# Flamingo-style gated cross-attention block on one core: the set-up becomes steps of the order tables

## The reference

```
h  = layernorm(x)
a  = ln1(h + mha(h, h, h, mask_s))              # unit A
b  = ln2(a + mha(a, ctx, ctx, mask_x))          # unit B
c  = ln3(b + relu(b @ w1 + b1) @ w2 + b2)       # C
x1 = x + tanh(g_x) * c
n  = layernorm(x1)
y  = x1 + tanh(g_f) * down(silu(gate(n)) * up(n))   # E: activations rounded to 8 bits, weights to -1, 0, 1
```

## Time and profile before

| | |
|---|---|
| median of 3 runs | 1021.93 us (1019.71 to 1024.56) |
| profiled execution | 1026.44 us, span 1024.5 us |
| PE busy | 867.8 us, 85% of the span |
| DVE busy | 788.5 us, 77% |
| ACT busy | 637.9 us, 62% |
| POOL busy | 591.2 us, 58% |
| mean granted TensorE clock | 0.934 |

### The profile page before, as it was taken

The page is one execution under the profiler, slowest core; times in us unless marked ns, Lnnn a source line. Parts: engine busy times, 40 slices in busy tenths (PEclk is TensorE's granted clock), DMA queues, the critical chain, the costliest instruction groups (busy, mean ns, idle before and its releaser), DMA issues.

```text
span 1024.5 us, 26372 instructions
## 1 busy us (share of the span) xinstructions
PE 867.8 (85%) x10089; PEld 708.1 (69%) x10147; DVE 788.5 (77%) x1903; ACT 637.9 (62%) x996; POOL 591.2 (58%) x630
## 2 busy tenths in 40 slices
PE   0327678989999999999999999999999999978565
PEld 0215457777878787878787878787878787766443
DVE  7654566668888888888888888888888888867454
ACT  1125254647677777777777767777777777764433
POOL 7004245566666666676767675757585858471520
PEclk9956696999999999999999999999999999989785
DMA  6251434343434343443444434343535352121000
GB/s 178 83 113 43 83 74 75 84 74 74 90 80 90 79 91 79 82 88 75 94 74 96 74 90 79 85 86 79 90 75 85 85 84 73 25 68 18 21 11 10
DMA packets 131755, 77.71 MB, mean 76 GB/s; under 512 B 10121, under 2 KB 131120, under 8 KB 131633
## 3 DMA queue, kind: packets, MB, share of 16 engines
q1 hardware_dynamic: 131632, 76.04, 36.7%
HBM read 54.49 MB, written 20.98 MB: 74 GB/s over the span
## 4 chain that ended last, share of the span: by engine, by line
PE 44%; DVE 16%; POOL 13%; DMA 10%; SPq 7%; issue 6%; ACT 3%; POOLq 0%; DVEq 0%; ACTq 0%
DMA stk_AQ<-parts_AQ 9%; PE lin_C L671 7%; SPq L583 6%; PE lin_A L671 4%; PE lin_E L671 4%; PE lin_B L671 4%; POOL elo L1343 3%; PE smax L750 3%; PE st L774 3%; DVE lst L1112 3%; POOL lrs L1323 2%; POOL late L1374 2%; PE smax L746 2%; POOL late L1366 2%; DVE nm_A L1162 2%
## 5 line engine op out<-in xcount | busy, mean ns | idle before, releaser
L1343 POOL TENSOR_TENSOR elo<-e,ehi 128x1024 f16<-128x1024 f32 x128 | 273.8, 2139 | 149.7 <-ACT ehi L943 149.4
L1323 POOL TENSOR_TENSOR lrs<-lve,neghalf 128x1 f32<-128x1 f32 (+1 forms) x112 | 70.9, 633 | 199.8 <-DVE lve L1121 195.5
L941 ACT ACTIVATE e<-st 128x1024 f32<-128x1024 f32 x128 | 130.1, 1017 | 45.1 <-PE st L774 44.0
L943 ACT ACTIVATE ehi<-st 128x1024 f16<-128x1024 f32 x128 | 129.8, 1014 | 0.0
L1162 DVE TENSOR_REDUCE nm_B<-smax 128x4 f32<-128x512 f32 x128 | 87.6, 684 | 20.0 <-PE smax L750 19.9
L1162 DVE TENSOR_REDUCE nm_A<-smax 128x4 f32<-128x512 f32 x128 | 87.7, 685 | 19.2 <-PE smax L750 18.5
L671 PE MATMUL lin_C<-w,late 128*128 128x256 f16 x768 | 90.0, 274 | 0.0
L671 PEld LDWEIGHTS lin_C<-w,late 128*128 128x128 f16 x768 | 75.7, 99 | 8.8
L746 PE MATMUL smax<-mb,ident_big 128*128 128x512 f16 x128 | 52.2, 408 | 18.5 <-DMA stk_AQ<-parts_AQ 9.8
L750 PE MATMUL smax<-stk_BK,stk_BQ 126*128 126x128 f16 x512 | 50.7, 222 | 9.0 <-DVE nm_B L1162 5.9
L750 PEld LDWEIGHTS smax<-stk_AK,stk_AQ 126*128 126x128 f16 x512 | 42.2, 102 | 18.3 <-issue 4.1
(11 more groups left out here) (284 smaller groups left out, 2827.3 us busy)
## 6 DMA issues: line engine op xcount, KB each, us to landing
stk_AK<-parts_AK SPq DMA_DIRECT2D x64, 128.0 KB, 4.0
stk_AQ<-parts_AQ SPq DMA_DIRECT2D x64, 128.0 KB, 5.6
stk_BK<-parts_BK SPq DMA_DIRECT2D x64, 128.0 KB, 3.7
stk_BQ<-parts_BQ SPq DMA_DIRECT2D x64, 128.0 KB, 3.7
x_a<-in_x_dram SPq DMA_DIRECT2D x16, 256.0 KB, 2.8
cx<-in_ctx_dram SPq DMA_DIRECT2D x16, 256.0 KB, 2.7
parts_AK<-qk_AK SPq DMA_DIRECT2D x16, 256.0 KB, 2.2
parts_AQ<-qk_AQ SPq DMA_DIRECT2D x16, 256.0 KB, 2.5
```

Of the source, the lines that this page charges most:

```text
L941: eng.activation(e32[:, hf, :], st[:, :], ACT.Exp, scale=SCORE).then_inc(e32_ready, 1)
L943: eng.activation(ehi[:, hf, :], st[:, :], ACT.Exp, scale=SCORE).then_inc(st_drained, 1)
L1323: eng.tensor_tensor(lrs[n][:, a:b], lve[n][:, a:b], neghalf[:, 0:b - a], ALU.pow).then_inc(ln_rstd[n], 1)
L1343: eng.tensor_tensor(elo[:, hf, :], e32[:, hf, :], ehi[:, hf, :], ALU.subtract).then_inc(elo_ready, 1)
```

## The change

- The set-up has no straight program any more but for a few constants. `PREPARE` names its steps ("set", ...), 44 of them, all of group 0, and `AT`, `LATE` and `BANK` give them places beside the first groups' steps. Each weight has its own step and its own semaphores; the first use of each result in group 0 waits for it.
- SP loads x, then two weights, the masks, the context and the others. The eight bias loads are issued by ScalarE's queue, to 22 partitions of 128 numbers instead of one row of 2816; two VectorE operations split them, and they go through DRAM into `brows`. The value-bias products are not added to the row but written into two further rows of `brows`.
- Memsets of the stacks' constant rows run over 32-bit words: a pair of f16 numbers packed in one.
- `TWEAK` adds delays to steps of single groups: 0, 1, 2 and 13, 14, 15. In group 15 the E steps get 4.97 to 8.34. All of `AT`, `START`, `LATE` and `BANK` is new.

The diff, cut to its core:

```diff
+PREPARE = (
+    [("set", n) for n in ("const", "rows", "mask", "flags", "gate", "scales")]
+    + [("set", "w", n) for n in range(10)] + [("set", "load", n) for n in range(9, 13)] + [("set", "bv", i) for i in range(2)]
+    + [("set", "stk", s, t) for s in "AB" for t in "QK"]
+    + [("set", n, m) for n in ("abs", "mean", "scale", "clip") for m in range(3)]
+    + [("set", "turn", m, r) for m in range(3) for r in range(2)]
+)
...
-START = [0.0000, 1.0125, 2.0274, 3.0405, 4.0533, 5.0678, 6.0803, 7.0946, 8.1074, 9.1216, 10.1358, 11.1490, 12.1628, 13.1762, 14.1912, 15.2043]
+START = [0.0000, 1.0188, 2.0283, 3.0470, 4.0636, 5.0814, 6.1004, 7.1147, 8.1321, 9.1501, 10.1674, 11.1867, 12.2041, 13.2212, 14.2296, 15.2538]
...
 def place(engine, item):
     g, step = item
-    if step[0] == "setup":
-        return SETUP_AT[g, step[1]]
-    return START[g] + AT[step] + LATE.get((engine, step), 0.0)
+    return START[g] + AT[step] + LATE.get((engine, step), 0.0) + TWEAK.get(item, 0.0)
...
+        bq = e32[0:NROW, 0, 0:P]
+        def pair(value):
+            return struct.unpack("<f", struct.pack("<ee", value, value))[0]
...  SP
             eng.dma_start(x_a[:, :, :], x_v[0]).then_inc(x_in, 16)
-            eng.dma_start(cx[:, :, :], ctx_v[0]).then_inc(cx_in, 16)
+            load(1)
+            load(0)
...
-            eng.wait_ge(u_b1, N_BIAS)
-            eng.dma_start(brows[0:1, :], bhi).then_inc(u_w, 16)
-            eng.dma_start(brows[1:2, :], blo).then_inc(u_w, 16)
...
+                elif what == "rows":
+                    eng.wait_ge(u_split, 2)
+                    for q, part in enumerate((bhi, blo)):
+                        eng.dma_start(brow_dram[q].rearrange("(r c) -> r c", c=P), part).then_inc(u_rows, 16)
+                    eng.wait_ge(u_const, N_CONST)
+                    eng.wait_ge(u_rows, 32)
+                    eng.dma_start(brows[0:2, :], brow_dram).then_inc(u_brow, 16)
...
+                elif what == "load":
+                    for k in {9: range(4), 10: range(4, 8), 11: (8,), 12: (9,)}[n]:
+                        eng.wait_ge(u_lo[k], 1)
+                    if n < 11:
+                        bv = ("set", "bv", n - 9)
+                        eng.wait_ge(filled[lane_of(bv)], count(lane_of(bv), 0, bv))
+                    load(n)
...  TensorE
-            eng.wait_ge(u_const, N_CONST)
+            eng.wait_ge(u_const, N_FIRST)
...
+                    if g == 0:
+                        eng.wait_ge(u_brow, 16)
+                        eng.wait_ge(u_lo["AB".index(s) * 4 + "QK".index(name)], 1)
...
-            eng.wait_ge(u_lo, 8)
-            eng.wait_ge(u_dve, 13)
-            eng.wait_ge(u_w, 48)
...  ScalarE
+            for name, width in BIASES:
+                r = BCOL[name] // P
+                eng.dma_start(bq[r:r + width // P, :], w[name].rearrange("(r c) -> r c", c=P)).then_inc(u_bias, 16)
...  VectorE
-            setup(eng.tensor_scalar(bf[:, 0:last], bf[:, 0:last], WS, None, ALU.mult), u_b1, n_b1)
-            setup(eng.tensor_scalar(bf[:, last:NBIAS], bf[:, last:NBIAS], WS * WS, None, ALU.mult), u_b1, n_b1)
-            setup(eng.tensor_copy(bhi, bf), u_b1, n_b1)
-            setup(eng.tensor_tensor(blo, bf, bhi, ALU.subtract), u_b1, n_b1)
+                elif what == "rows":
+                    eng.wait_ge(u_bias, 16 * len(BIASES))
+                    setup(eng.tensor_scalar(bhi, bq, WS, None, ALU.mult), u_split, 1)
+                    eng.scalar_tensor_tensor(blo, bq, WS, bhi, ALU.mult, ALU.subtract).then_inc(u_split, 1)
...
+                if what == "stk" and n == "A":
+                    rows = stk["A", r][:, :, :].rearrange("p h n -> p (h n)").bitcast(F32)
+                    a, b = ((rows[MROW:P, :], 0.0), (rows[MROW:MROW + 1, :], pair(BIG))) if r == "Q" else (
+                        (rows[MROW:96, :], 0.0), (rows[96:P, :], pair(MS)))
```

More of the change, by code:

```diff
@@ L18 @@
+import struct
 from contextlib import ExitStack
@@ new lines @@
+    ("set", "rows")): -0.0404, ("DVE", ("set", "flags")): -0.1114, ("DVE", ("set", "gate")): 0.0017, ("DVE",
+    ("set", "scales")): 0.0088, ("DVE", ("set", "w", 0)): -0.0476, ("DVE", ("set", "w", 1)): 0.0013, ("DVE",
+    ("set", "w", 2)): -0.3080, ("DVE", ("set", "w", 3)): -0.0991, ("DVE", ("set", "w", 4)): 0.0639, ("DVE",
+    ("set", "w", 5)): -0.2167, ("DVE", ("set", "w", 8)): 0.7753, ("DVE", ("set", "w", 9)): -0.2253, ("DVE",
+    ("set", "bv", 0)): -0.0021, ("DVE", ("set", "stk", "A", "K")): 0.1051, ("DVE", ("set", "abs", 0)): 0.2689,
@@ L229, in idle @@
 def idle(engine, step):
+    if step[0] == "set":
+        return engine == "ACT"
     if engine == "ACT":
@@ L250, in half @@
     return halves // 2
-def jobs_before(bank, m, part):
-    here = ORDER["PE"].index((m, ("setup", part)))
-    return sum(1 for item in ORDER["PE"][:here] if lane_of(item[1]) == bank)
 def check_order():
@@ L312, in check_order @@
         before("DVE", g, ("E", "amax"), ("E", "norm"), g + 1)
-    for m in range(3):
-        for part in range(4):
-            before("PE", m, ("setup", part), ("C", "T"), 0)
-            for e in ENGINES:
-                before(e, m, ("setup", part), ("setup", (part + 1) % 4), m + (part == 3))
+    for e in ENGINES:
+        for what in ("abs", "mean", "scale", "clip"):
+            for m in range(2):
+                before(e, 0, ("set", what, m), ("set", what, m + 1), 0)
+        for m in range(3):
+            before(e, 0, ("set", "turn", m, 0), ("set", "turn", m, 1), 0)
+            if m < 2:
+                before(e, 0, ("set", "turn", m, 1), ("set", "turn", m + 1, 0), 0)
+                before(e, 0, ("set", "turn", m, 1), ("set", "clip", m + 1), 0)
+        before(e, 0, ("set", "bv", 0), ("set", "bv", 1), 0)
+    before("DVE", 0, ("set", "turn", 2, 1), ("set", "scales"), 0)
+    before("DVE", 0, ("set", "gate"), ("set", "scales"), 0)
+    before("POOL", 0, ("set", "const"), ("set", "stk", "B", "Q"), 0)
 BIASES = [("s_bq", D), ("s_bk", D), ("c_bq", D), ("c_bk", D), ("ff_b1", F), ("s_bo", D), ("c_bo", D), ("ff_b2", D)]
@@ L599, in _ @@
                 what, name = step[0:2]
-                if what == "setup":
-                    if name == 1 and g < 2:
-                        late_load(11 + g)
+                if what == "set":
+                    prepare(*step[1:3])
                 elif name in ("inK", "inQ"):
@@ new lines, in prepare @@
+            def prepare(st_, what, n=0, r=0):
+                bank, fill, drain, before, after = st_.job()
+                wait(eng, drain, before)
+                if what == "flags":
+                    eng.wait_ge(u_dve, 10)
+                    eng.transpose(bank[:, :].bitcast(F16)[:, 0:P], mb[:, :], ident16[:, :])
+                    eng.matmul(bank[:, P:2 * P], ones[:, :], scr[:, :], start=True, stop=True, skip_group_check=True)
+                    mm = eng.matmul(bank[:, 2 * P:2 * P + NB], ones[0:NB, :], scr2[0:NB, 0:NB], start=True, stop=True,
+                                    skip_group_check=True)
+                elif what == "bv":
+                    eng.wait_ge(u_bvb, n + 1)
+                    eng.wait_ge(u_raw[4 * n + 3], 16)
+                    for c in range(DC):
+                        mm = eng.matmul(bank[:, 0:D], bvb[:, c, :], raw[4 * n + 3][:, c * D:(c + 1) * D],
+                                        start=(c == 0), stop=(c == DC - 1))
+                elif what == "mean":
+                    eng.wait_ge(u_abs, n + 1)
+                    mm = eng.matmul(bank[:, 0:1], ones[:, :], rs3[:, n:n + 1], start=True, stop=True)
+                else:
+                    eng.wait_ge(u_const, N_CONST)
+                    eng.wait_ge(u_clip, 2 * n + 2)
+                    half_bank = bank[:, :].bitcast(BF16)
+                    for k in range(8):
+                        blk = r * 8 + k
+                        mm = eng.transpose(half_bank[:, k * P:(k + 1) * P], wq16[:, blk * P:(blk + 1) * P], identb[:, :])
+                mm.then_inc(fill, 1)
@@ new lines, in prepare @@
+            def prepare(what, n=0):
+                if what == "w":
+                    dst = (wp[wmats[n][0], wmats[n][1]] if n < 8 else (w1p, w2p)[n - 8])[0]
+                    eng.wait_ge(u_raw[n], 16)
+                    eng.activation(dst[:, :, :].rearrange("p c n -> p (c n)"), raw[n], ACT.Copy, scale=WS).then_inc(u_hi[n], 1)
+                elif what == "bv":
+                    eng.wait_ge(u_bv, 32)
+                    if n:
+                        eng.wait_ge(filled[lane_of(("set", "bv", 0))], count(lane_of(("set", "bv", 0)), 0, ("set", "bv", 0)))
+                    for c in range(DC):
+                        a_ = eng.activation(bvb[:, c, :], ones[:, :], ACT.Copy, scale=bvcol[:, n, c:c + 1])
+                    a_.then_inc(u_bvb, 1)
+                elif what == "gate":
+                    eng.wait_ge(u_g, 32)
@@ L894, in ternary @@
                     eng.activation(tanhx[:, :], graw[:, 0:1], ACT.Tanh).then_inc(u_act, 1)
```

(22 more changed lines are left out.)

428 lines of the change are left out of this document (230 added, 198 removed), and 243 rows, old and new, of tables (AT, BANK, LATE, TWEAK).

## The result

The changed kernel takes 994.65 us (median of 4 runs, 991.99 to 998.65) against 1020.82 for the kernel before beside it (4 runs): a ratio of 0.974, 95% interval 0.970 to 0.979. Forecast were 1001, with 983 to 1015 as the range. The profiled execution took 995.81, its span is 993.9. First the stretches, in the columns of the earlier trace rows.

A forecast was written before the change was run, and what follows sets the result against it. TensorE was taken to bound the middle, with order and waits pacing the fill and TensorE not the bound at either end; -21 fill, +2 middle and -2 tail gave -21, so 1021.9 becomes about 1001, range 983 to 1015.

The forecast's parts named there:

- Set-up: Before group 0's first maximum: statistics at 27.7 instead of 38.87, normalisation at 30.5, lead 11.1, then 7.3 more, making 18.4.
- The lock: VectorE's two-port operations and GpSimd exclude each other; an overlap at the mask would cost one word memset, 1.76 us.
- just covered: Before group 0's first maximum: stacks issued by 47.3 land by 53, when clips and turns end at 53.1.
- 2.1 won: First to second group: K and Q ahead of the scores, so the stack issue follows them by 4.8 for 11.5.
- 0.5: Group 2: a further 0.5 us added to the lead, as lumps of set-up are spread there.
- Waits of group 0 alone add nothing later: Middle: waits that only group 0 has cost the later groups nothing.
- Rival (b): From 50 to 125: denser fill brings the 2.4 GHz clock sooner, saving about 15 busy us, half on the chain: 994; chance 0.13.
- Rival (a): Fill: only the first lead stays, moved steps costing the same between groups 0 and 1's maxima: 11 of lead, 1011; chance 0.17.
- +2, near zero because every step and wait stays: Middle groups: swapped neighbours lose 2 us in total, with bounds of 15 either way.
- Rival (c): Middle: beat lengthens as VectorE's X and values step wait for the Q stack's landing; at 2.6 per group 1028; chance 0.05.
- -2: Tail: O split ahead of group 14's statistics and second F2 ahead of down products win 2 us, between 0 and 4.
- Delays of group 15's E steps: 0: Tail: delaying group 15's E steps costs 0, as nothing is queued behind them.

The follow-up runs named there:

- the set-up alone: Changed kernel's split set-up, with places, banks and starts of ordinary steps as in the kernel before and no delays: 1008.92 us for 1021.48 beside it.
- both loads back: Changed kernel with the context load and C's x load back in SyncE's order of before, in groups 2 to 12: 989.96 us.
- without the end delays: Changed kernel without the delays of steps in groups 13, 14 and 15, their starts evenly spaced: 1006.45 us.

## Why the prediction was right, and where its sum was not

**Direction and size**: right, 994.65 for 1001, inside the range. But its terms were further off than their sum. In the profiles the lead is 30.6 for 21: 10.6 more by group 4 and 3.9 more in the tail, less 4.9 more lost in the middle. The medians show 26.2. That the time came out within 6.4 of the forecast is in part luck.

**Set-up**: right up to group 0's normalisation, too good behind it. Statistics 25.98 (26 to 30 asked for), no mask operation over 2, first maximum 55.43 (50 to 56), group 1's Q stack issued by 85.8 (86 to 93, just missed). GpSimd's memsets end at 14.87 and VectorE comes to the mask at 15.55, as counted. The lock was looked for there and was paid elsewhere, in the power, for 1.9; as the statistics were 1.7 early, the normalisation stood at 30.63 for 30.5 by luck. From there to the first maximum it took 24.8 for 22.6. K's split ended at 43.8 for 42.8, and the landing of the stacks, forecast as just covered, seems not to have been: VectorE's last turn ends at 53.7, the products for the maximum start at 54.38, and the last K transfer, issued at 47.7, landed near 54 by my estimate, as these take 5.1 to 6.4. So the lead there was 16.1, not 18.4. Alone the set-up is worth 12.6 by the medians, 16.4 by the two profiles.

**First groups**: this step failed. "2.1 won", "0.5" for lumps, and "Waits of group 0 alone add nothing later". From the first maximum to group 1's Q stack issued it took 30.3, where 36.2 was forecast and 38.3 it was before, and the lead of 16.1 became 24.0 at group 1 and 29.4 at group 2. From the set-up alone to the changed kernel the lead grows by 4.2 at group 1 and by 11.7 at group 5. I had counted one swap, K and Q ahead of the scores, and taken the rest of the first groups' delays for small change. They are worth 25.4 in this kernel and make that swap too; the new places without any delays cost 22.9 alone.

**Rival (b)**, 994 from the clock, has the right time, but as far as the runs tell not the cause: from 83 to 92 the higher clock alone won 0.9 and nothing in the total. From 50 to 75 it stays open. **Rival (a)** falls: the lead grew behind the first maximum instead of shrinking to 11.

**Middle**: the step "+2, near zero because every step and wait stays" was mis-sized: 6.9 in the profile, 4.7 between the medians of the changed kernel and of the one with both loads back. The beat of 53.15 also missed the sign asked for, 52 to 53. TensorE's waits for the B unit's stacks did not stay: 0.4 became 5.4. The swaps were listed with the context load on SyncE among them, but C's x load, which had also passed the max row, was not; without that one put back the waits stay. Rival (c) named a longer beat, and VectorE as its place: the beat grew by 0.6, not 2.1, and not there.

**Tail**: -2 was mis-sized too, 5.9 in the profile, though the last F2 is read 37 before the end (956.75; 36 asked for). The wait for the O split went as forecast, by means of the small delays, which do the rest as well, and "Delays of group 15's E steps: 0" holds for the large ones.

**What stays open**: which of the small delays carry the gain, one by one, whether C's x load alone makes up the loss in the middle, and what the clock is worth between 50 and 75.

## What to carry to other kernels

In an order written out by hand, places and corrections are one thing: price them together, and look first for what stands at the head of an in-order queue waiting, ahead of work that others need. A lead at the start is for the most part handed on where a chain has a fixed beat, so shorten the set-up; then read the steady state again for each transfer that was moved, not only for the compute. A large transfer that is wanted late should not be issued right ahead of transfers that are wanted now.

## What the runs showed of the hardware

- With a load of 256 KB issued 0.5 ahead of four loads of 128 KB, these took 4.0 and 4.1 from issue to landing (median of 44 in two kernels), 3.6 and 3.7 without it, and TensorE's waits for them were 5.4 and 6.0 over eleven groups, 0 and 0.4 without it. Their four issues took 1.82 to 3.77 with it and 1.82 to 2.85 in the kernel with both loads back.
- GpSimd's power of 128x2 elements took 2.63 beside a VectorE operation of 2.28 with two inputs in SBUF, 0.72 otherwise.
- The same instructions ran at either clock in different executions. K's last six products of group 0 in the changed kernel take 1.49 at 40.93 (above); without the end delays, with the same program up to there, they take 0.82, and the first row maximum is at 53.42 instead of 55.43:

```profile
39.69 0.82 PE L740 MATMUL lin_E<-hT_A,w_AK 128*128 128x256 f16 x6
```

- The granted clock of a stretch reads 1.00 from 25 to 75 in the changed kernel although six products take 1.49 up to 40.93 and twelve 2.77 at 64.35; without the end delays, where products are rather faster, it reads 0.89 from 25 to 50 and 0.70 from 50 to 75. Here the durations are the better witness.
- A memset of f16 pairs written as 2048 words took 1.76 on VectorE for zero and for two packed constants, where 4096 f16 elements took 3.47.
